# A four-layer attention kernel: a unit's score banks in the first layer filled and read in two pairs, under a new order of work

## The reference

```python
q = layer_norm(transpose(zt_prev + pos), ln_q_g, ln_q_b)
kv = layer_norm(transpose(za + pos), ln_kv_g, ln_kv_b)
Q, K, V = split(q @ Wq), split(kv @ Wk), split(kv @ Wv)
attn = einsum('bhqd,bhkd->bhqk', Q, K) / sqrt(8)
ctx = einsum('bhqk,bhkd->bhqd', softmax(attn), V)
r = ctx_merged @ Wo + q
out = r + gelu(layer_norm(r) @ W1 + b1) @ W2 + b2
```

## Time and profile before

| | |
|---|---|
| median of 3 runs | 2175.59 us (2171.83 to 2178.16) |
| profiled execution, its own time | 2173.42 us |
| its span | 2171.6 us |
| first and last exponentials of the first layer | start at 37.15 and 315.1 us |
| PE, PEld busy | 95%, 79% of the span |
| DVE, ACT, POOL busy | 67%, 59%, 31% of the span |
| granted TensorE clock over the span | 0.987 of full speed |

### The profile page before, as it was taken

The page is one execution under the profiler, slowest core; times in us unless marked ns, Lnnn a source line. Parts: engine busy times, 40 slices in busy tenths (PEclk is TensorE's granted clock), DMA queues, the critical chain, the costliest instruction groups (busy, mean ns, idle before and its releaser), DMA issues. The chain is left out here.

```text
span 2171.6 us, 47506 instructions
## 1 busy us (share of the span) xinstructions
PE 2064.9 (95%) x17700; PEld 1719.2 (79%) x17700; DVE 1455.5 (67%) x2808; ACT 1283.3 (59%) x3304; POOL 676.6 (31%) x681
## 2 busy tenths in 40 slices
PE   6999979999898899999999999999998999999899
PEld 4666646888687788888888888888887877777788
DVE  5777754555455576666677866666676449999953
ACT  4777764566653555445455554544555549998853
POOL 4444411111124423030212403030101238888811
PEclk9999999999999999999999999999999999999999
DMA  4000001000001223232322323232222120000000
GB/s 140 17 17 12 2 13 48 2 2 2 27 15 61 86 83 110 85 101 90 98 96 86 100 81 102 82 110 72 72 74 99 62 60 2 2 2 2 2 16 25
DMA packets 119007, 117.16 MB, mean 54 GB/s; under 512 B 6656, under 2 KB 91136, under 8 KB 117760
## 3 DMA queue, kind: packets, MB, share of 16 engines
q1 hardware_dynamic: 118784, 114.13, 16.5%
HBM read 78.72 MB, written 35.39 MB: 53 GB/s over the span
## 5 line engine op out<-in xcount | busy, mean ns | idle before, releaser
L866 ACT ACTIVATE l_probs<-l_s_psum,l_neg_max 128x129 f32<-128x129 f32 x512 | 183.3, 365 | 299.4 <-DVE l_neg_max L948 299.4
L953 DVE SCALAR_TENSOR_TENSOR l_context_low<-l_c_psum,cols,l_context_high 128x512 fp32r<-128x512 f32 x128 | 95.9, 749 | 186.1 <-ACT l_context_high L861 185.9
L690 POOL TENSOR_TENSOR l_head_w_high<-l_head_raw,one 128x768 fp32r<-128x768 f32 x30 | 44.7, 1490 | 481.6 <-PE l_t_psum L823 464.4
L1503 DVE TENSOR_REDUCE l_neg_max<-l_psum 128x2 f32<-128x512 f32 x256 | 162.5, 683 | 35.7 <-PE l_psum L1293 34.6
L2587 POOL TENSOR_TENSOR l_probs<-l_probs,l_mask_add 128x512 f32<-128x512 f32 x128 | 163.5, 1288 | 37.0 <-DVE l_probs L2818 36.6
L1432 ACT ACTIVATE l_PT<-l_psum 128x512 f32<-128x512 f32 x256 | 132.2, 602 | 58.2 <-PE l_psum L1321 57.1
L2758 ACT ACTIVATE l_probs<-l_probs,l_neg_max 128x128 f32<-128x128 f32 x512 | 160.9, 396 | 9.6 <-DVE l_neg_max L2825 9.3
L805 PEld LDWEIGHTS l_c_psum<-l_PT,values 128*128 128x128 f32 x1024 | 135.4, 194 | 19.1 <-DMA l_PT<-l_moving 8.0
L805 PE MATMUL l_c_psum<-l_PT,values 128*128 128x128 f32 x1024 | 137.5, 278 | 5.9 <-DMA l_PT<-l_moving 5.9
L782 PE MATMUL l_s_psum<-l_KT,l_QT 128*128 128x129 f32 x1024 | 135.1, 274 | 2.4 <-issue 1.6
L973 DVE TENSOR_TENSOR x<-x,l_o_psum 128x512 f32<-128x512 f32 x128 | 87.9, 687 | 70.4 <-PE l_o_psum L823 70.4
(11 more groups left out here) (329 smaller groups left out, 6309.4 us busy)
## 6 DMA issues: line engine op xcount, KB each, us to landing
l_moving<-l_turned SPq DMA_DIRECT2D x127, 256.0 KB, 2.0
l_PT<-l_moving SPq DMA_DIRECT2D x508, 64.0 KB
l_head_raw<-in_l_heads SPq DMA_DIRECT2D x32, 384.0 KB, 4.5
l_w<-in_l_w SPq DMA_DIRECT2D x4, 1024.0 KB, 10.5
l_ctx_in<-in_ctx_T SPq DMA_DIRECT2D x16, 256.0 KB, 5.4
l_value_raw<-in_l_values SPq DMA_DIRECT2D x8, 512.0 KB, 5.1
l_value_rows<-in_l_rows SPq DMA_DIRECT2D x8, 512.0 KB, 6.0
l_x_in<-in_x_T SPq DMA_DIRECT2D x16, 128.0 KB, 2.2
```

Source lines behind the costliest of these rows:

```text
L866: last = act.activation(probs[:, i, :], scores[:, i // 2, i % 2, :], ACT.Exp, bias=neg_max[:, i:i + 1], scale=1.0, accum_out=den[:, i:i + 1])
L953: dve.scalar_tensor_tensor(out=context[1][:, :], in0=c_bank[:, :], scalar=vector("bias_v", s), in1=context[0][:, :].bitcast(F32), op0=ALU. ...
L1503: dve.tensor_reduce(neg_max[:, u % 2, qt, at:at + 2], bank[:, :].rearrange("p (e k) -> p e k", e=2), AX, ALU.max, negate=True).then_inc(fr ...
```

## The change

A quarter's matmuls are given out in two parts. Part 2z fills banks 0 and 1 from row groups 0 and 1, part 2z+1 fills banks 2 and 3 from groups 2 and 3, each followed by a `score_full` increment of its own. The first part waits for two fewer exponentials (`- 2 + 2 * pair`), the second for all of the quarter before. ACT waits for `score_full` before exponentials 0 and 2 of a quarter. The guards on `score_full` elsewhere count 8 to a unit for 4.

All times in `AT0` are new too. In a unit PE now runs: score parts 0 and 1, rows 0 and 1, renormed, untangle 0, score part 2, rows 2 and 3, score part 3, rows 4 to 6, normed, untangle 1, score part 4, row 7, score part 5, rows 8 and 9, context 0, context_T, score part 6, rows 10 and 11, score part 7, rows 12 and 13, out, project, rows 14 and 15, context 1, neg_T, back, value. ACT runs: exponentials 0 to 3, renormed_a, 4 to 7, normed_a, 8 to 11, slots 0, turned_T, 12 to 15, project_a, scaled, neg_T_a, back_a, slots 1. On DVE, share, added, scaled_b, stats and values stand at other places between the maxima. POOL runs root_b, parts, round, place, root, blocks in this order, where place was the last of them and for one unit later.

```diff
--- before.py
+++ after.py
@@ -1013,40 +1013,40 @@
 
 
 AT0 = {
-    "place": (-5.673,),
-    "stats": (-3.0107,),
-    "root": (-4.0246,),
-    "scaled": (-2.1776,),
-    "normed": (-2.3861,),
-    "normed_a": (-1.9233,),
-    "project": (-1.8672,),
-    "project_a": (-1.201,),
-    "round": (-2.1985,),
-    "blocks": (-1.7725,),
-    "value": (-1.5283,),
-    "values": (-1.1004,),
-    "rows": (-1.4052, -1.402, -1.3555, -1.2623, -1.2258, -1.2055, -1.158, -1.0944, -1.0721, -1.0458, -0.9634, -0.945, -0.9245, -0.9035, -0.8251, -0.7736),
-    "maximum": (-0.9638, -0.8484, -0.7911, -0.7547, -0.7051, -0.6529, -0.6276, -0.6149, -0.5456, -0.498, -0.4294, -0.4102, -0.3484, -0.3016, -0.1933, -0.1312),
-    "parts": (-1.363,),
-    "neg_T": (-0.7105,),
-    "neg_T_a": (-0.0985,),
-    "score": (-0.434, -0.2839, -0.0823, 0.0678),
-    "exponents": (-0.0603, -0.0048, 0.0078, 0.0143, 0.1012, 0.1146, 0.2115, 0.2215, 0.2315, 0.2534, 0.2826, 0.3839, 0.5302, 0.5915, 0.6823, 0.7585),
-    "context": (0.0312, 0.2496),
-    "slots": (0.4996, 0.9345),
-    "untangle": (0.6089, 0.7574),
-    "share": (1.1849, 1.2895),
-    "context_T": (1.0677,),
-    "turned_T": (1.5067,),
-    "out": (1.1168,),
-    "added": (1.8023,),
-    "back": (1.4395,),
-    "back_a": (1.9293,),
-    "stats_b": (2.1696,),
-    "root_b": (1.6338,),
-    "scaled_b": (2.6486,),
-    "renormed": (2.655,),
-    "renormed_a": (3.0848,),
+    "place": (-4.7141,),
+    "stats": (-2.8966,),
+    "root": (-3.5526,),
+    "scaled": (-2.2168,),
+    "normed": (-2.0861,),
+    "normed_a": (-1.6961,),
+    "project": (-1.6622,),
+    "project_a": (-1.3193,),
+    "round": (-1.8108,),
+    "blocks": (-1.5286,),
+    "value": (-1.5013,),
+    "values": (-0.7855,),
+    "rows": (-1.4558, -1.4509, -1.3402, -1.3215, -1.217, -1.1887, -1.1421, -1.0263, -0.9253, -0.8999, -0.7377, -0.7086, -0.6809, -0.68, -0.6208, -0.5864),
+    "maximum": (-0.7855, -0.7205, -0.6752, -0.6604, -0.6163, -0.6053, -0.6007, -0.5108, -0.4925, -0.4289, -0.2101, -0.1975, -0.1851, -0.1486, -0.1356, 0.0755),
+    "parts": (-0.8269,),
+    "neg_T": (-0.5188,),
+    "neg_T_a": (-0.1621,),
+    "score": (-0.4905, -0.4861, -0.3568, -0.3195, -0.0503, 0.0704, 0.2483, 0.3027),
+    "exponents": (-0.0017, 0.0341, 0.0803, 0.0805, 0.1509, 0.2051, 0.2369, 0.3029, 0.3492, 0.4396, 0.4618, 0.4626, 0.5438, 0.5715, 0.643, 0.6538),
+    "context": (0.1419, 0.4416),
+    "slots": (0.5165, 0.9317),
+    "untangle": (0.5717, 0.9191),
+    "share": (1.2948, 1.4412),
+    "context_T": (1.222,),
+    "turned_T": (1.5257,),
+    "out": (1.3299,),
+    "added": (1.8575,),
+    "back": (1.495,),
+    "back_a": (1.9146,),
+    "stats_b": (2.1399,),
+    "root_b": (1.6289,),
+    "scaled_b": (2.7162,),
+    "renormed": (2.5499,),
+    "renormed_a": (3.1241,),
 }
 
 
@@ -1210,7 +1210,7 @@
             def make_blocks(u):
                 emptied(pool, "project", u)
                 if u >= 2:
-                    pool.wait_ge(score_full, 4 * (u - 2) + 4)
+                    pool.wait_ge(score_full, 8 * (u - 2) + 8)
                 shape = [P, 4, KEYS]
                 q = Q[:, u % 2, :].unsqueeze(1).to_broadcast(shape)
                 own = c.halves(8).unsqueeze(2).to_broadcast(shape)
@@ -1303,20 +1303,21 @@
                                         c.ident_bf[:, :])
                 last.then_inc(full, 1)
 
-            def score(u, z):
+            def score(u, part):
+                z, pair = part // 2, part % 2
                 w, t = quarter(z)
-                if z == 0:
+                if part == 0:
                     pe.wait_ge(blocks_done, u + 1)
                     emptied(pe, "neg_T", u)
                 if u or z:
-                    pe.wait_ge(exp_done, 4 * (4 * u + z))
+                    pe.wait_ge(exp_done, 4 * (4 * u + z) - 2 + 2 * pair)
                 for e in range(2):
-                    for g in range(4):
+                    for g in range(2 * pair, 2 * pair + 2):
                         at = slice(32 * g, 32 * g + 32)
                         pe.matmul(score_banks[g][:, e * KEYS:(e + 1) * KEYS], K[at, u % 2, t * P:(t + 1) * P],
                                   blocks[at, u % 2, 2 * w + e, :], start=True, stop=False,
                                   tile_position=(32 * g, 0))
-                    for g in range(4):
+                    for g in range(2 * pair, 2 * pair + 2):
                         at = slice(32 * g, 32 * g + 32)
                         last = pe.matmul(score_banks[g][:, e * KEYS:(e + 1) * KEYS],
                                          c.select8[at, 2 * w + e:2 * w + e + 1].to_broadcast([32, P]),
@@ -1409,7 +1410,7 @@
                 if u >= 2:
                     act.wait_ge(blocks_done, u - 1)
                     act.wait_ge(blocks_rounded, u - 1)
-                    act.wait_ge(score_full, 4 * (u - 2) + 4)
+                    act.wait_ge(score_full, 8 * (u - 2) + 8)
                     filled(act, "rows", u - 2, 15)
                 act.activation(Q[:, u % 2, :], bank[:, 0:KEYS], ACT.Copy, scale=8.0 ** -0.5)
                 act.activation(K[:, u % 2, :], bank[:, KEYS:], ACT.Copy)
@@ -1419,14 +1420,15 @@
                 bank, full, free, k = work("neg_T", u)
                 act.wait_ge(full, k + 1)
                 if u >= 2:
-                    act.wait_ge(score_full, 4 * (u - 2) + 4)
+                    act.wait_ge(score_full, 8 * (u - 2) + 8)
                 act.activation(neg_T[:, u % 2, :], bank[:, :].bitcast(BF16)[:, 0:KEYS], ACT.Copy).then_inc(free, 1)
 
             def exponents(u, part):
                 z, g = part // 4, part % 4
                 w, t = quarter(z)
+                if g % 2 == 0:
+                    act.wait_ge(score_full, 2 * (4 * u + z) + g // 2 + 1)
                 if g == 0:
-                    act.wait_ge(score_full, 4 * u + z + 1)
                     if u:
                         filled(act, "context", u - 1, w)
                 act.activation(PT[:, 2 * w + t, g, :], score_banks[g][:, :], ACT.Exp).then_inc(exp_done, 1)
```

## The result

The changed kernel takes 2182.32 us (median of 6 runs, 2178.8 to 2187.46) against 2174.49 us for the kernel before in the same series: the ratio is 1.0036, 95% interval 1.0022 to 1.0049. It is slower by 0.36%, which a measurement can just tell from no change. I had forecast 2159, with 2150 to 2175 as the range and 0.10 for slower. The profiled execution has a span of 2177.0 us, 5.4 more than before; the last exponentials of the first layer start at 321.6 us for 315.1. So the loss arises in the layer that was changed.

A forecast was written before the change was run, and what follows sets the result against it. PE and ACT taking turns, then PE's order, were taken to bound the unit. 15 unit steps x 1.2 = -18.0 us, last unit -1.2, +3 for stalls: -16.2, so 2159 us, range 2150 to 2175.

The forecast's parts named there:

- What bounds the kernel: First layer's unit: turns of PE and ACT set 0 to 7.05 us, PE's order 7.05 to 14.25, then maxima, POOL's parts, neg_T.
- The pair at the second quarter: Its first part starts after two exponentials, at 2.5 us for 3.52; its exponentials start at 4.08 for 4.93, -0.85 us.
- The step that failed: On PE's queue a quarter's second part passes the first part's queued work and starts at most 0.36 us late.
- The strict order: Rival, chance 0.07: second part starts when the first has ended, row jobs wait for it; unit 20.9 us, kernel 2222.
- the queue looks only half a part ahead: Rival, chance 0.11: second parts and row jobs beside first parts start 0.54 us late, 1.15 us a unit; 2176.
- half the gain stays: Rival, chance 0.15: maxima 13 to 15 come 0.6 us later, so neg_T does too; 9 us less gain, 2168.
- Moved steps: place ahead of root on POOL, stats ahead of values on DVE: cost nothing, bounds 0 and +0.2 us a unit.
- My walk: Step times through one unit of the first layer, ending with the next unit at 16.6 us for 17.82, -1.2 us.

The follow-up runs named there:

- mixed: Changed kernel with row jobs ahead of scores and only the second quarter in two parts, the others whole: 2156.02 us, ratio 0.9936 to the kernel before.
- the probes: Changed kernel without the bf16 matmuls that add the negative maxima (2155.56 us), with one-pass scores from rounded copies (2154.12 us), or with parts given out group by group (2246.05 us).
- the two probes: Changed kernel without the bf16 matmuls that add the negative maxima (2155.56 us), and with scores computed from rounded copies in one pass (2154.12 us).

## Why the prediction was wrong

The times of the steps, in us from the unit's first score, as read from the rows:

| step | before | predicted | after | mixed |
|---|---|---|---|---|
| second quarter | 3.52 | 2.5 | 2.64 | 2.55 |
| its exponentials | 4.93 | 4.08 | 4.03 | 3.94 |
| third quarter | 7.05 | 6.1 | 6.67 | 6.37 |
| first context | 8.57 | 7.75 | 8.73 | 7.89 |
| fourth quarter | 11.24 | 10.0 | 10.96 | 10.14 |
| row jobs 14 and 15 | 14.25 | 13.0 | 14.86 | 13.15 |
| neg_T | 16.92 | 15.7 | 17.54 | 15.83 |
| next unit | 17.81 | 16.6 | 18.43 | 16.72 |

- **What bounds the kernel: right.** The turns of PE and ACT set the first stretch, PE's order the middle, and from row jobs 14 and 15 to the next unit it is 3.56 or 3.57 us in the three measured columns, 3.6 in the predicted one.
- **The pair at the second quarter: right.** -0.9 us at its exponentials after the change, for the -0.85 forecast.
- **The step that failed** is "I take it that the second part passes those of the first. It then starts at most 0.36 us late". The second part does pass part of the first one's work, but what stands behind a first part, second part or row job, starts 0.54 to 0.55 us late at every quarter. At the first this hardly shows: the second quarter starts at 2.64 for 2.5. Second to third takes 4.03 us for my 3.6, third to context 2.06 for 1.65, fourth to out 2.27 for 1.6. That is 0.43 + 0.41 + 0.67 of the 1.8 us between 16.6 and 18.43. The mixed kernel, in which the second quarter alone is still in parts, needs 3.82, 1.52 and 1.52 for these three.
- **Why it failed.** The second layer's rows did show a matmul passing over a dozen records, but of several groups. I took the total for the limit; by the probes the limit is each group's own. A row job there leaves six records waiting in its group, a part leaves ten. The evidence was of the right kind and four records short. The strict order was wrong too: after the change the second part's first half runs beside the first part's second half (181.63), and the unit is 18.4 us, not 20.9.
- **The rival that came nearest** is "the queue looks only half a part ahead", to which I gave 0.11: its 0.54 us are the measured 0.55. I priced it at no change (2176). That its delay fits is in part luck: as a rule it is refuted by the two probes, in which the second part starts after 0.03 us. For the rest of the way to 2182 the runs show a candidate, occupied work banks: 0.2 us of waiting before normed, 0.2 before untangle, 0.3 each before the weights of project and of a row job. From out to row jobs 14 and 15 the unit takes 1.63 us for 1.50 before. How much of the loss is the banks' alone was not measured. It is not what my rival "half the gain stays" said: that had the last maxima late before neg_T, and from row jobs 14 and 15 to neg_T it is 2.68 us for 2.67. I had treated late parts and waits on maxima as alternatives; both are there.
- **Moved steps: as costed.** place, root, stats and values show no wait in the mixed kernel, which has them where the changed one has.
- **Sizes.** From the first exponentials of the layer to those of the last unit the profile has 7.5 us more than before; that is less than 15 x 0.6, since the first steps and the last one grew less. The last unit is 0.9 us shorter (11.1 us from its first to its last exponentials, for 12.0), where I said 1.2. So the last exponentials are 6.5 us later, the span is 5.4 longer, and the medians differ by 7.8. My walk also lost 0.1 us: out at 11.6 and 1.5 "as now" make 13.1 for row jobs 14 and 15, not 13.0.

The mixed kernel stays close to the walk that was meant for the changed one, 16.7 us for 16.6. In part that is luck, for it is another order: second to third quarter takes 0.2 us longer than in the walk, third to context and fourth to out 0.2 less together. Its profile has a span 22.3 us shorter than before and last exponentials 17.9 us earlier, its median is 15.0 us lower; the difference was not looked into.

## What to carry to other kernels

When you count on independent row groups running side by side, count how many records of one group stand ahead of the first record of another; a total over groups misled me here. Put short work of a free group ahead of long work, and split a fill in two only where its reader would otherwise wait. When a change moves producers, follow the buffers that they fill: here the waits for work banks grew from 0.2 to 0.9 us a unit when row jobs came late.

## What the runs showed of the hardware that I had not expected

- A part given out group by group ran its two groups 0.54 us apart, 2246 us for the kernel in its one run, and the unit was 21.7 us: the order of sixteen instructions was worth some 64 us. In the kernel before, which changes the group at every instruction, four groups start together (eight f32 records from 177.41).
- "TensorE: Matmul & The Clock Gate" of the Trainium skill (Part 3, on packing small matmuls) has matmuls in strict program order. In the probe without the bf16 matmuls the second part's f32 matmuls start 0.03 us after the first part's and before most of them; in the mixed kernel the fourth quarter starts 0.01 us after row jobs that have a second matmul still to run. Order across row groups is not strict here; by the strict rule the unit would have been 20.9 us in my estimate, and it was 18.4.
